# Selective-scan kernel: both sums of the softplus moved from VectorE to TensorE and PSUM

## The chip, the cores and the metric
The kernel runs on one core of one Trainium2 chip. The time is the device time of that core in microseconds (us). Five engines run their own instruction streams and meet through semaphores: TensorE (PE, matmuls), VectorE (DVE), ScalarE (ACT), GpSimd (POOL) and SyncE (SP, which starts DMAs).

## The reference, cut to what matters
A Mamba layer (8 sequences of 512 tokens, width 256, state 16) is followed by a layer norm and a mixture of 8 experts. What the change touches is `dt`, one number per token and channel, and what reads it:

```
dt = softplus(x_conv @ dt_w.T + dt_b)           # softplus(v) = relu(v) + ln(1 + exp(-|v|))
dA = exp(dt * A)                                # 16 states per channel
h  = h * dA + (dt * B) * x                      # the scan over tokens
y  = sum over states of h * C  + x * D
```

The kernel adds a correction to the logarithm. With e = exp(-|v|) it rounds t = e + 1 and keeps rest = (t - 1) - e, so that dt = relu(v) + ln(t) - rest. Three arrays of 128x1024 (two halves of 128 channels beside each other, 512 tokens each) therefore have to be summed for every sequence: `relu`, `logp` and `rest`.

## The kernel before, in words
**Stages.** Stage 1 computes the Mamba layer, the norms and the routing, one sequence at a time, and lasts until about 580 us. Stage 2 runs the experts, tile by tile, and stage 3 is the last norm. Only stage 1 is touched.

**Rounds and slots.** Stage 1 is a loop over rounds `r.like` = -1 (`FIRST`) to 9 (`LAST`), and in a round over 16 slots `t`, one for each state (`SLOTS`, `for r in ROUNDS: for t in range(SLOTS)`). Every engine walks through the same rounds and slots in its own function (`pe_stage1`, `act_stage1`, `dve_stage1`, `pool_stage1`) and issues in each slot what belongs to it. This order is written by hand; nothing else plans it. The engines are not in the same slot at the same time: each goes on as far as its semaphores allow. In round k four sequences are at work: part `a` prepares sequence k+1 (projections, convolution, softplus), part `b` scans sequence k, part `c` projects and norms sequence k-1, and part `d` routes sequence k-2. Part `c` starts in round 1, part `d` in round 2. `FIRST` has part `a` alone, round 7 has no part `a`.

**The scan.** In slot t DVE multiplies the drive by B (`weigh_inputs`, L1042, twice) and scans (`scan`, L1051, twice); POOL multiplies the state of slot t-1 by C (`read_state`, L1187, into `read`); PE adds the `read` of slot t-2 into `p_y` through the identity (`sum_states`, L640); ACT makes the decays of slot t+2 (`decays`, L824). The drive itself, `p_u` = dt * x_conv, is one DVE instruction in slot 15 (`drive`, L1033), and slot 0 of the next round reads it.

**The softplus of sequence k+1 in round k.** ACT stores |v| and relu(v) in slot 8 (L789, L790), then B and C (`store_bc`, L815), computes exp and t in slot 9 (L796, L800) and the logarithm in slot 10 (L806; it loads another table for it). DVE computes `rest` in slot 11 (`softplus_rest`, L1011), adds relu and logp in slot 12 (`add_log`, L1018), and subtracts `rest` in slot 13 (`scan_inputs`, L1025), which gives `dt`. POOL's `while_scanning` waits in slots 11, 12, 13 and 15 for these four DVE instructions before it goes on to its own `read_state`. In `FIRST` the same is done once, before the first scan.

**PSUM banks.** Every product of parts a, c and d goes through one of two banks in turn (`Round.blocks` lists them in order). PE fills a bank, signals `bank_full`, ACT or DVE copies it out and signals `bank_read`; PE may fill it again when the block before in that bank is read.

**What else stands near.** On ACT: the squares of the second norm (`variance`, L853) in slot 11, the copy of the gate's second half (`store_in`, L762) in slot 12, the second norm (`second_norm`, L861) in slot 13, the SiLU of the gate (`silu_gate`, L782) with two table loads in slot 14. On POOL: the power of the second norm (`power`, L1202 to L1206) in slot 12, and indirect DMAs that scatter rows (`scatter`, L1229) in slots 2 to 15, two of them at the start of slot 15. At the start of a round PE transposes and routes (`transpose_rows`, `route`), projects (`project`), counts (`count`, which DVE reads at L1106), projects out and convolves.

Of the kernel before, what the change touches and what calls it, by code (L numbers as in the profile page):

```python
# [53 lines left out]
class Round:  # L54
# [13 lines left out]
    def blocks(self):  # L68
        d, a, c = self.d, self.a, self.c
        return (["tr0", "tr1", "rt"] * d + ["in0", "in1"] * a + ["cnt"] * d + ["o0", "o1"] * c + ["cv0", "cv1"] * a  # L70
                + ["dt0", "dt1", "bc", "in2", "in3"] * a)

    def block(self, name):

# [79 lines left out]
def build(nc, ctx, ins, out):  # L154
    def sem(name):
        return ctx.enter_context(nc.semaphore(name))

    def sb(name, *shape, dt=F32, at=ctx):
        return at.enter_context(nc.sbuf_tensor(name, [P, *shape], dt))
# [23 lines left out]
    for name, *shape in SMALL:  # L183
# [39 lines left out]
    c_before, ones_f, b_out = set_up[:, 0:P], set_up[:, P:2 * P], set_up[:, 2 * P:2 * P + D]  # L223
    reorder = sb("reorder", P, at=one)
    table = sb("table", 1, at=one)
    rate_t = sb("rate_t", HALVES, P, at=one)
    rate = sb("scan_rate", HALVES, STATE, at=one)
    skip_w = sb("skip_w", HALVES, P, at=one)
# [46 lines left out]
    s_xt, s_x = sem("s_xt"), sem("s_x")  # L275
    bank_full = [sem(f"bank_full{i}") for i in range(2)]
    bank_read = [sem(f"bank_read{i}") for i in range(2)]
    s_silu, s_exp, s_log, s_rest0, s_rest, s_sum, s_dt, s_u = (
        sem(n) for n in ("s_silu", "s_exp", "s_log", "s_rest0", "s_rest", "s_sum", "s_dt", "s_u"))
    s_put = [sem(f"s_put{i}") for i in range(2)]  # L280
    s_rep = [sem(f"s_rep{i}") for i in range(RING)]
    s_order, s_decay, s_bu, s_state, s_read, s_added = (
# [284 lines left out]
    def pe_stage1(pe):  # L567
# [57 lines left out]
        def from_xc(r, name, at, n):  # L625
# [2 lines left out]
                pe.wait_ge(s_silu, 2 * r.s.at(1).n + 1)  # L628
            product(bank[0:n, :], columns(at, n), lambda k: xc[r.s.at(1).p][:, k, :]).then_inc(done, 1)

        def sum_states(s, t):

            n = SLOTS * s.n + t
            if t == 0:
                after(pe, s_y, s.n)
                for h in range(HALVES):
                    pe.matmul(p_y[h][:, :], skip_w[:, h, :], xc[s.p][:, h, :], start=True, stop=False)
            pe.wait_ge(s_read, n + 1)
            for h in range(HALVES):
                mm = pe.matmul(p_y[h][:, :], ident[:, :], read[:, t % 4, h, :], start=False, stop=(t == SLOTS - 1))  # L640
            mm.then_inc(s_added, 1)
# [49 lines left out]
        for r in ROUNDS:  # L691
            for t in range(SLOTS):
                if t < 2 and r.c:
                    sum_states(r.s.at(-1), SLOTS - 2 + t)
                if r.last and t == 0:
                    transpose_tile(pe, Seq(0, 0))
                    up_projection(pe, Seq(0, 0), 0)
                if r.d and t == 0:
                    transpose_rows(r, 0)
                    transpose_rows(r, 1)  # L700
                if r.d and t == 1:
                    route(r)
                if r.a and t == 2:
                    project(r, 0)
                    project(r, 1)
                if r.last and t == 4:
                    up_projection(pe, Seq(0, 0), 1)
                if r.d and t == (4 if r.last else 3):
                    count(r)
                if r.c and t == 3:  # L710
                    project_out(r, 0)
                    project_out(r, 1)
                if r.a and t == 4:
                    convolve(r, 0, range(TAPS))
                if r.a and t in (5, 6):
                    half = TAPS // 2 * (t - 5)
                    convolve(r, 1, range(half, half + TAPS // 2))
                if r.like == Round.FIRST and t == 5:
                    order_rate()
                if r.a and t == 8:  # L720
                    for i in range(HALVES):
                        from_xc(r, f"dt{i}", DT_ + i * P, P)
                    from_xc(r, "bc", BC, 2 * STATE)
                if r.like == Round.FIRST and t == 9:
                    place_rate()
                if r.a and t in (10, 11):
                    project(r, t - 8)
                if t >= 2 and r.b:
                    if t == 2 and r.like == 0:
                        pe.wait_ge(s_set_dve, SET_DVE)  # L730
                    sum_states(r.s, t - 2)


    def act_stage1(act):
# [49 lines left out]
        def store_dt(r, h):  # L784

            bank, done = full(act, r, f"dt{h}")
            if h == 0 and r.b:
                act.wait_ge(s_dt, r.s.n + 1)
            act.activation(relu[:, h, :], bank[:, :], ACT.Relu, bias=b_dt[:, h:h + 1])  # L789
            act.activation(expo[:, h, :], bank[:, :], ACT.Abs, bias=b_dt[:, h:h + 1]).then_inc(done, 1)  # L790

# [23 lines left out]
            act.activation(bc_out[0:2 * STATE, :], bank[0:2 * STATE, :], ACT.Identity, bias=b_bc2[0:2 * STATE, 0:1])\  # L815
               .then_inc(done, 1)

        def decays(s, t):

            after(act, s_state, halves_done(s, t - AHEAD))  # L820
            if t == 0:
                act.wait_ge(s_dt, s.n + 1)
            for h in range(HALVES):
                act.activation(decay[t % AHEAD][:, h, 1:LEN], dt[s.p][:, h, 1:LEN], ACT.Exp, scale=rate[:, h, t:t + 1])\  # L824
                   .then_inc(s_decay, 1)
# [43 lines left out]

        def store_x1t(r, k):  # L870
            bank, done = full(act, r, f"tr{k}")
            act.wait_ge(s_sum, SEQS if not r.a else r.s.n + 1)
            act.activation(x1t[:, k, :], bank[:, :], ACT.Copy).then_inc(done, 1)

        def router_exp(r):
# [4 lines left out]
        for r in ROUNDS:  # L880
            for t in range(SLOTS):
# [15 lines left out]
                if r.a and t in (11, 12):  # L897
                    store_in(r, t - 9)
                if r.a and t == 14 and r.b:
                    silu_gate(r)  # L900
                if r.like == 0 and t == 2:
                    silu_gate(Round(r.s.at(-1), Round.FIRST))

                if r.like == Round.FIRST and t == SLOTS - 1:
                    act.wait_ge(s_set_dve, SET_DVE)
                    for i in range(AHEAD - 2):
                        decays(r.s.at(1), i)
                if r.b and t < SLOTS - AHEAD + 2:
                    decays(r.s, t + AHEAD - 2)
                if r.next_b and r.b and t >= SLOTS - AHEAD + 2:  # L910
                    decays(r.s.at(1), t - SLOTS + AHEAD - 2)
                if r.a and r.b and t == 10:
                    softplus_log(r)

# [65 lines left out]
    def dve_setup_rest(dve):  # L980
        dve.memset(neg_half[:, :], -0.5)
        for i, value in enumerate((-1.0 / (16 * D), -1.0 / D, EPS)):
            dve.memset(norm_c[:, i, :], value)
        dve.tensor_copy(base[:, :], c_queue[:, :])
        dve.tensor_scalar(lower[:, :, :], lower[:, :, :], -SMALLEST, None, ALU.mult)
        dve.tensor_copy(before[:, :], c_before)
        dve.tensor_copy(ones[:, :], ones_f)
        dve.memset(scrap[:, 2:3], 0.0).then_inc(s_left, 1)
        dve.memset(chosen[:, :, :], 0.0)
        for h in range(HALVES):  # L990
            dve.tensor_scalar(skip_w[:, h, :], ident[:, :], skip[:, h:h + 1], None, ALU.mult)
        for h in range(2):
            last = dve.memset(rows[h][:, :, :], 0.0)
        last.then_inc(s_set_dve, 1)
        for i in range(AHEAD):
            last = dve.memset(decay[i][:, :, 0:1], 0.0)
        last.then_inc(s_set_dve, 1)
# [6 lines left out]
    def dve_stage1(dve):  # L1004
# [6 lines left out]
            dve.scalar_tensor_tensor(flat(rest[:, :, :]), flat(rest[:, :, :]), -1.0, flat(expo[:, :, :]),  # L1011
                                     ALU.add, ALU.subtract).then_inc(s_rest, 1)

        def add_log(r):

            s = r.s.at(1)
            dve.wait_ge(s_log, s.n + 1)
            dve.tensor_tensor(flat(relu[:, :, :]), flat(relu[:, :, :]), flat(logp[:, :, :]), ALU.add).then_inc(s_sum, 1)  # L1018

        def scan_inputs(r):  # L1020

            s = r.s.at(1)
            dve.wait_ge(s_sum, s.n + 1)
            dve.wait_ge(s_rest, s.n + 1)
            dve.tensor_tensor(flat(dt[s.p][:, :, :]), flat(relu[:, :, :]), flat(rest[:, :, :]), ALU.subtract).then_inc(s_dt, 1)  # L1025

        def drive(r):

            s = r.s.at(1)
            dve.wait_ge(s_dt, s.n + 1)  # L1030
            dve.wait_ge(s_silu, 2 * s.n + 1)
            after(dve, s_bu, halves_done(s, -1))
            dve.tensor_tensor(p_u[:, :], flat(dt[s.p][:, :, :]), flat(xc[s.p][:, :, :]), ALU.mult).then_inc(s_u, 1)  # L1033
# [88 lines left out]
        for r in ROUNDS:  # L1122
            for t in range(SLOTS):
# [36 lines left out]
                    dve.tensor_copy(index[r.s.at(-2).p][:, :], flat(spot_sum[:, :, :])).then_inc(s_index, 1)  # L1160
                if r.a and t == (11 if r.b else 10):
                    softplus_rest(r)
                if r.a and t == (12 if r.b else 10):
                    add_log(r)
                if r.like == Round.FIRST and t == 11:
                    negate_rate(dve)
                if r.a and t == 13:
                    scan_inputs(r)
                if r.c and t == 9:
                    residual(r)  # L1170
                if r.a and t == SLOTS - 1:
# [7 lines left out]
    def pool_stage1(pool):  # L1179
# [57 lines left out]
        def while_scanning(r, t):  # L1237
# [5 lines left out]
                pool.wait_ge(s_index, r.s.at(-2).n + 1)  # L1243
            if r.a and t == 11:
                pool.wait_ge(s_rest, r.s.at(1).n + 1)
            if r.a and t == 12:
                pool.wait_ge(s_sum, r.s.at(1).n + 1)
            if r.c and t == 9:
                pool.wait_ge(s_residual, r.s.at(-1).n + 1)
            if r.a and t == 13:  # L1250
                pool.wait_ge(s_dt, r.s.at(1).n + 1)
            if r.a and t == 15:
                pool.wait_ge(s_u, r.s.at(1).n + 1)

# [446 lines left out]
```

## Time and profile before

| what | value |
|---|---|
| median of 3 timed runs | 1333.25 us (1333.24 to 1339.11) |
| the profiled execution's own time | 1337.31 us |
| its span, first to last instruction | 1335.5 us |
| mean granted clock of TensorE | 0.941 |
| busy: PE, DVE, ACT, POOL | 88%, 79%, 67%, 56% of the span |
| drive of the first sequence starts | 39.30 us |
| drive of the seventh (last in round 6) starts | 506.60 us |

Times in the rows are microseconds from the start of the span. A matmul of f32 shows as two records, so that 8 records of L640 are the four matmuls of two slots. Records of neighbouring instructions overlap a little, because a record includes the tail of an instruction; the distance of two starts is what an instruction takes in a full queue. "Idle before" in square brackets is the time that the engine stood still before the row, with the instruction that ended it.

### The profile page before, as it was taken

To read this page: it belongs to the slowest core of one execution; us is meant where nothing else is said; L and a number is where in the kernel's file an instruction comes from. 1 tells how busy PE (TensorE), PEld (TensorE's weight loads), DVE (VectorE), ACT (ScalarE), POOL (GpSimd) and SP (SyncE) were. 2 spreads that over 40 slices of the span, in tenths; PEclk is the share of its full clock that TensorE was granted. 3 is DMA by queue.
4 is the path that set the end of the run, shared out by engine and by line. 5 is a ranking of instruction groups with operands and counts; after the bars stand their busy time and mean duration, and the time that the engine had idled before them with its cause. 6 is when DMAs were issued, how large, how long until landed. Compare 5 with 4: busy or idle time off the path is not lost. (4 is left out here: it accounts for less than half of the span.)

```text
span 1335.5 us, 17897 instructions
## 1 busy us (share of the span) xinstructions
PE 1170.2 (88%) x5138; PEld 805.3 (60%) x5138; DVE 1048.7 (79%) x1791; ACT 896.6 (67%) x1551; POOL 745.3 (56%) x566
## 2 busy tenths in 40 slices
PE   7879897979898897676899999999999999999940
PEld 3324353534353434245788888888888888888830
DVE  2999999999999999964777667777677777766734
ACT  3785959495959585516577766777676777766734
POOL 0356567888787878967633444443444433444442
PEclk9899998999999898977899999999999999999975
DMA  2543444445454545354866556556556566556637
GB/s 74 217 179 127 154 148 177 176 166 187 173 191 172 192 154 181 127 192 157 315 164 161 133 139 165 160 162 162 128 140 167 160 162 163 138 135 161 162 36 252
DMA packets 69260, 217.21 MB, mean 163 GB/s; under 512 B 7520, under 2 KB 43232, under 8 KB 56288
## 3 DMA queue, kind: packets, MB, share of 16 engines
q1 hardware_dynamic: 29664, 167.42, 34.4%
q0 software_dynamic: 26880, 36.72, 16.1%
q10 hardware_dynamic: 12672, 12.58, 2.9%
q8 instruction: 16, 0.26, 0.1%
q14 instruction: 28, 0.23, 0.0%
HBM read 165.54 MB, written 51.15 MB: 162 GB/s over the span
## 5 line engine op out<-in xcount | busy, mean ns | idle before, releaser
L640 PE MATMUL p_y<-read,small 128*128 128x512 f32 x512 | 257.8, 642 | 58.2 <-POOL read L1187 58.2
L1051 DVE TENSOR_TENSOR_SCAN state<-decay,p_bu 128x512 f32<-128x512 f32 x256 | 297.3, 1203 | 1.5 <-issue 1.5
L1511 POOL DMA_INDIRECT total<-o_v,tok x144 | 267.4, 1857 | 44.1 <-issue 44.0
L640 PEld LDWEIGHTS p_y<-read,small 128*128 128x128 f32 x512 | 101.3, 205 | 199.5 <-issue 116.8
L1509 POOL TENSOR_TENSOR scrap<-neg_half 128x1 f32<-128x1 f32 x36 | 13.6, 379 | 319.9 <-ACT o_v L1418 317.3
L824 ACT ACTIVATE decay<-dt,scan_rate 128x511 f32<-128x511 f32 x256 | 164.3, 710 | 10.1 <-DVE state L1051 9.8
L504 ACT ACTIVATE gate_v<-p_g,bias 128x512 f32<-128x512 f32 x144 | 98.4, 683 | 102.8 <-PE p_up L494 97.7
L1229 POOL DMA_INDIRECT queues<-rows,index x128 | 133.4, 1042 | 32.5 <-issue 29.2
L1405 ACT ACTIVATE ah<-a_v 128x512 fp32r<-128x512 f32 x144 | 91.1, 633 | 89.6 <-DVE a_v L518 85.9
L1187 POOL TENSOR_TENSOR read<-state,bc 128x1024 f32<-128x1024 f32 x64 | 127.5, 2004 | 20.7 <-DVE p_bu L1042 8.4
L512 DVE TENSOR_SCALAR up_v<-up_v 128x512 f32<-128x512 f32 x144 | 61.4, 427 | 68.5 <-ACT up_v L507 65.9
L1456 DVE TENSOR_TENSOR al<-a_v,ah 128x512 fp32r<-128x512 f32 x144 | 98.8, 686 | 12.4 <-ACT ah L1405 12.4
L518 DVE SCALAR_TENSOR_TENSOR a_v<-gate_v,up_v 128x512 f32<-128x512 f32 x144 | 99.7, 693 | 4.9
L507 ACT ACTIVATE up_v<-p_up,bias 128x512 f32<-128x512 f32 x144 | 98.2, 682 | 0.0
L1187 POOL TENSOR_TENSOR read<-state,first_wh 128x1024 f32<-128x1024 f32 x32 | 64.0, 2001 | 59.6 <-DVE p_bu L1042 53.8
L1187 POOL TENSOR_TENSOR read<-state,first_wl 128x1024 f32<-128x1024 f32 x32 | 63.9, 1997 | 39.9 <-DVE p_bu L1042 15.6
L1378 PE MATMUL p_o<-first_wh,ah 128*128 128x256 f32 x288 | 82.6, 287 | 2.3 <-DVE al L1456 2.3
L1378 PE MATMUL p_o<-wh,ah 128*128 128x256 f32 x288 | 81.9, 284 | 1.7 <-DVE al L1456 1.7
L1042 DVE TENSOR_TENSOR p_bu<-p_u,bc 128x512 f32<-128x512 f32 x128 | 81.3, 681 | 0.0
L1378 PE MATMUL p_o<-first_wl,ah 128*128 128x256 f32 x288 | 80.8, 281 | 0.0
L1378 PE MATMUL p_o<-first_wh,al 128*128 128x256 f32 x288 | 80.8, 281 | 0.0
L1378 PE MATMUL p_o<-wh,al 128*128 128x256 f32 x288 | 80.3, 279 | 0.0
(220 smaller groups left out, 3017.6 us busy)
## 6 DMA issues: line engine op xcount, KB each, us to landing
bc<-bc_rows SPq DMA_DIRECT2D x32, 1024.0 KB, 4.7
first_raw<-in_w_experts SPq DMA_DIRECT2D x19, 1668.0 KB
raw_w<-in_w_experts SPq DMA_DIRECT2D x18, 1668.0 KB
first_wh<-bc_rows SPq DMA_DIRECT2D x16, 1024.0 KB
first_wl<-bc_rows SPq DMA_DIRECT2D x16, 1024.0 KB
first_rows<-queues SPq DMA_DIRECT2D x19, 544.0 KB
xq<-queues SPq DMA_DIRECT2D x18, 544.0 KB
queues<-pad SPq DMA_DIRECT2D x9, 544.0 KB
```

The lines of the kernel that those rows point to most:

```text
L504: act.activation(gate_v[i % 2][:, :], p_g[i % 2][:, :], ACT.Silu, bias=bias[t.p][:, 0, i:i + 1], scale=ALPHA)
L507: act.activation(up_v[i % 2][:, :], p_up[i % 2][:, :], ACT.Identity, bias=bias[t.p][:, 1, i:i + 1])\
L518: dve.scalar_tensor_tensor(a_v[i % 2][:, :], gate_v[i % 2][:, :], TOP, up_v[i % 2][:, :], ALU.min, ALU.mult)\
L640: mm = pe.matmul(p_y[h][:, :], ident[:, :], read[:, t % 4, h, :], start=False, stop=(t == SLOTS - 1))
L824: act.activation(decay[t % AHEAD][:, h, 1:LEN], dt[s.p][:, h, 1:LEN], ACT.Exp, scale=rate[:, h, t:t + 1])\
L1051: dve.tensor_tensor_scan(state[t % 4][:, h, :], decay[t % AHEAD][:, h, :], p_bu[:, h * LEN:(h + 1) * LEN], 0.0, ALU.mult, ALU.add).then_in ...
L1187: pool.tensor_tensor(read[:, t % 4, :, :], state[t % 4][:, :, :], of_state(t, 1), ALU.mult).then_inc(s_read, 1)
L1229: pool.indirect_dma_start(queues, bass.IndirectOffsetOnAxis(ap=index[s.p][:, i:i + 1], axis=0), rows[s.p][:, i // TOPK, :], None).then_inc ...
L1378: mm = pe.matmul(to, v[:, i, a * P:(a + 1) * P], w[t.p][:, c:c + D], start=(i == 0 and a % 2 == 0 and m == 0), stop=(i == CH - 1 and m == ...
L1405: act.activation(ah[:, i, :], a_v[i % 2][:, :], ACT.Copy).then_inc(s_ah, 1)
L1456: dve.tensor_tensor(al[:, i, :], a_v[i % 2][:, :], ah[:, i, :].bitcast(F32), ALU.subtract).then_inc(s_al, 1)
L1511: pool.indirect_dma_start(total, bass.IndirectOffsetOnAxis(ap=tok[t.p][:, a:a + 1], axis=0), o_v[t.p][:, a, :], None, compute_op=ALU.add). ...
```

## The change
DVE no longer adds. For each half PE runs three matmuls into a bank (two new blocks `sp0` and `sp1`): the identity times relu, the identity times logp, and minus the identity (`minus`, a new constant) times rest. It does so in slots 12 and 13, before that slot's `sum_states`. ACT copies both banks to `dt` in slot 14, and `silu_gate` moves from slot 14 to 15. DVE's drive, ACT's first decays and POOL wait accordingly: the semaphores `s_sum` and `s_dt` are gone, and with them POOL's waits in slots 12 and 13.

```diff
@@ blocks
-                + ["dt0", "dt1", "bc", "in2", "in3"] * a)
+                + ["dt0", "dt1", "bc", "in2", "in3", "sp0", "sp1"] * a)
@@ pe_stage1
+        def add_softplus(r, h):
+
+            s = r.s.at(1)
+            bank, done = block(r, f"sp{h}")
+            pe.wait_ge(s_log, s.n + 1)
+            if h == 0 and r.like == Round.FIRST:
+                pe.wait_ge(s_set_dve, SET_DVE)
+            pe.matmul(bank[:, :], ident[:, :], relu[:, h, :], start=True, stop=False)
+            pe.matmul(bank[:, :], ident[:, :], logp[:, h, :], start=False, stop=False)
+            pe.wait_ge(s_rest, s.n + 1)
+            pe.matmul(bank[:, :], minus[:, :], rest[:, h, :], start=False, stop=True).then_inc(done, 1)
@@
                 if r.a and t in (10, 11):
                     project(r, t - 8)
+                if r.a and t in (12, 13):
+                    add_softplus(r, t - 12)
@@ act_stage1: store_dt and store_x1t lose their waits on s_dt and s_sum
+        def store_sum(r, h):
+
+            s = r.s.at(1)
+            bank, done = full(act, r, f"sp{h}")
+            act.activation(dt[s.p][:, h, :], bank[:, :], ACT.Copy).then_inc(done, 1)
@@
-            if t == 0:
-                act.wait_ge(s_dt, s.n + 1)
+            if summed:
+                for h in range(HALVES):
+                    bank, n = summed.block(f"sp{h}")
+                    act.wait_ge(bank_read[bank], n)
@@
                 if r.a and t == 14 and r.b:
+                    store_sum(r, 0)
+                    store_sum(r, 1)
+                if r.a and t == 15 and r.b:
                     silu_gate(r)
@@
                 if r.like == Round.FIRST and t == SLOTS - 1:
                     act.wait_ge(s_set_dve, SET_DVE)
+                    store_sum(r, 0)
+                    store_sum(r, 1)
@@ dve_setup_rest
+        dve.tensor_scalar(minus[:, :], ident[:, :], -1.0, None, ALU.mult)
@@ dve_stage1: add_log (L1018) and scan_inputs (L1025) are gone
         def drive(r):
 
             s = r.s.at(1)
-            dve.wait_ge(s_dt, s.n + 1)
+            for h in range(HALVES):
+                bank, n = r.block(f"sp{h}")
+                dve.wait_ge(bank_read[bank], n)
@@ while_scanning (POOL)
-            if r.a and t == 12:
-                pool.wait_ge(s_sum, r.s.at(1).n + 1)
-            if r.a and t == 13:
-                pool.wait_ge(s_dt, r.s.at(1).n + 1)
```

## Rows read from the trace of the kernel before

**Rows 1.** The page's first part: busy time, share of the span, instructions.
```profile
PE 1170.2 (88%) x5138; PEld 805.3 (60%) x5138; DVE 1048.7 (79%) x1791; ACT 896.6 (67%) x1551; POOL 745.3 (56%) x566
```

**Rows 2.** Windows: length, busy PE, PEld, DVE, ACT, POOL, granted clock, DMA.
```profile
38.00:40.00 2.00, 1.75 (x3) 0.34 (x1) 1.97 (x4) 1.04 (x4) 0.00 (x0) 0.72 0.85 360
...
280.00:340.00 60.00, 52.80 (x153) 25.88 (x152) 57.84 (x81) 42.05 (x78) 48.63 (x38) 0.94 0.52 183
```

**Rows 3.** Waits of DVE, 230 to 437 us: total, times, longest.
```profile
DVE place L1106 <- PE p_bank L686: 2.6, 3, 0.9
DVE rest L1011 <- ACT rest L800: 2.1, 3, 0.7
```

**Rows 4.** Timeline of DVE: start, length, instruction, idle before.
```profile
39.30 1.23 DVE L1033 TENSOR_TENSOR p_u<-dt,xc 128x1024 f32<-128x1024 f32 x1
...
96.67 1.23 DVE L1033 TENSOR_TENSOR p_u<-dt,xc 128x1024 f32<-128x1024 f32 x1
...
162.41 1.23 DVE L1033 TENSOR_TENSOR p_u<-dt,xc 128x1024 f32<-128x1024 f32 x1
...
230.18 2.04 DVE L1033 TENSOR_TENSOR p_u<-dt,xc 128x1024 f32<-128x1024 f32 x1
...
355.76 1.23 DVE L1018 TENSOR_TENSOR first_raw<-first_raw,x1t 128x1024 f32<-128x1024 f32 x1 [0.16 <-ACT x1t L806]
356.90 2.32 DVE L1051 TENSOR_TENSOR_SCAN state<-decay,p_bu 128x512 f32<-128x512 f32 x2
...
360.32 1.22 DVE L1025 TENSOR_TENSOR dt<-first_raw,rest 128x1024 f32<-128x1024 f32 x1
...
368.52 2.05 DVE L1033 TENSOR_TENSOR p_u<-dt,xc 128x1024 f32<-128x1024 f32 x1
```

**Rows 5.** Timeline of POOL, columns as before.
```profile
154.88 0.60 POOL L1202 TENSOR_TENSOR rstd<-var,norm_c 128x4 f32<-128x4 f32 x1 [1.88 <-ACT squares L853]
...
360.99 0.60 POOL L1202 TENSOR_TENSOR rstd<-var,norm_c 128x4 f32<-128x4 f32 x1 [1.88 <-ACT squares L853]
...
365.49 3.97 POOL L1187 TENSOR_TENSOR read<-state,bc 128x1024 f32<-128x1024 f32 x2
369.63 1.80 POOL L1229 DMA_INDIRECT queues<-rows,index  x1 [0.17 <-issue]
371.73 0.98 POOL L1229 DMA_INDIRECT queues<-rows,index  x1 [0.30 <-DVE state L1051]
372.74 3.96 POOL L1187 TENSOR_TENSOR read<-state,bc 128x1024 f32<-128x1024 f32 x2
...
430.04 0.60 POOL L1202 TENSOR_TENSOR rstd<-var,norm_c 128x4 f32<-128x4 f32 x1 [1.88 <-ACT squares L853]
```

**Rows 6.** Timeline of PE, columns as before.
```profile
33.07 6.68 PE L597 MATMUL p_bank<-first_raw,w 128*128 128x512 f32 x8
...
100.08 5.58 PE L640 MATMUL p_y<-read,small 128*128 128x512 f32 x8 [2.85 <-POOL read L1187]
...
356.77 5.31 PE L640 MATMUL p_y<-read,small 128*128 128x512 f32 x12
367.56 6.69 PE L640 MATMUL p_y<-read,small 128*128 128x512 f32 x8 [5.47 <-POOL read L1187]
374.80 1.98 PE L640 MATMUL p_y<-read,small 128*128 128x512 f32 x4 [0.54 <-POOL read L1187]
...
552.93 1.98 PE L640 MATMUL p_y<-read,small 128*128 128x512 f32 x4 [2.83 <-POOL read L1187]
```

**Rows 7.** Timeline of ACT, columns as before.
```profile
348.19 0.68 ACT L815 ACTIVATE bc_out<-p_bank,b_bc 32x512 f32<-32x512 f32 x1 [0.84 <-PE p_bank L597]
...
360.82 0.67 ACT L762 ACTIVATE sg<-p_bank,small 128x512 f32<-128x512 f32 x1
...
363.84 2.06 ACT L861 ACTIVATE rows<-z,neg_mean,rstd 128x256 f32<-128x256 f32 x4
...
377.25 1.08 ACT L873 ACTIVATE x1t<-p_bank 128x512 f32<-128x512 f32 x2 [3.90 <-PE p_bank L664]
```

More of the change, by code:

```diff
@@ L225, in build @@
     table = sb("table", 1, at=one)
+    minus = sb("minus", P, at=one)
     rate_t = sb("rate_t", HALVES, P, at=one)
@@ L277, in build @@
     bank_read = [sem(f"bank_read{i}") for i in range(2)]
-    s_silu, s_exp, s_log, s_rest0, s_rest, s_sum, s_dt, s_u = (
-        sem(n) for n in ("s_silu", "s_exp", "s_log", "s_rest0", "s_rest", "s_sum", "s_dt", "s_u"))
+    s_silu, s_exp, s_log, s_rest0, s_rest, s_u = (
+        sem(n) for n in ("s_silu", "s_exp", "s_log", "s_rest0", "s_rest", "s_u"))
     s_put = [sem(f"s_put{i}") for i in range(2)]
@@ L786, in store_dt @@
             bank, done = full(act, r, f"dt{h}")
-            if h == 0 and r.b:
-                act.wait_ge(s_dt, r.s.n + 1)
             act.activation(relu[:, h, :], bank[:, :], ACT.Relu, bias=b_dt[:, h:h + 1])
@@ L816, in store_bc, with decays @@
                .then_inc(done, 1)
-        def decays(s, t):
+        def store_sum(r, h):
+            s = r.s.at(1)
+            bank, done = full(act, r, f"sp{h}")
+            act.activation(dt[s.p][:, h, :], bank[:, :], ACT.Copy).then_inc(done, 1)
+        def decays(s, t, summed=None):
             after(act, s_state, halves_done(s, t - AHEAD))
-            if t == 0:
-                act.wait_ge(s_dt, s.n + 1)
+            if summed:
+                for h in range(HALVES):
+                    bank, n = summed.block(f"sp{h}")
+                    act.wait_ge(bank_read[bank], n)
             for h in range(HALVES):
@@ L871, in store_x1t @@
             bank, done = full(act, r, f"tr{k}")
-            act.wait_ge(s_sum, SEQS if not r.a else r.s.n + 1)
             act.activation(x1t[:, k, :], bank[:, :], ACT.Copy).then_inc(done, 1)
@@ L905, in act_stage1 @@
                     act.wait_ge(s_set_dve, SET_DVE)
+                    store_sum(r, 0)
+                    store_sum(r, 1)
                     for i in range(AHEAD - 2):
-                        decays(r.s.at(1), i)
+                        decays(r.s.at(1), i, r if i == 0 else None)
                 if r.b and t < SLOTS - AHEAD + 2:
@@ L910, in act_stage1 @@
                 if r.next_b and r.b and t >= SLOTS - AHEAD + 2:
-                    decays(r.s.at(1), t - SLOTS + AHEAD - 2)
+                    decays(r.s.at(1), t - SLOTS + AHEAD - 2, r if t == SLOTS - AHEAD + 2 else None)
                 if r.a and r.b and t == 10:
@@ L1012, in softplus_rest @@
                                      ALU.add, ALU.subtract).then_inc(s_rest, 1)
[L1014 to L1025, printed above, removed]
         def drive(r):
             s = r.s.at(1)
-            dve.wait_ge(s_dt, s.n + 1)
+            for h in range(HALVES):
+                bank, n = r.block(f"sp{h}")
+                dve.wait_ge(bank_read[bank], n)
             dve.wait_ge(s_silu, 2 * s.n + 1)
@@ L1162, in dve_stage1 @@
                     softplus_rest(r)
-                if r.a and t == (12 if r.b else 10):
-                    add_log(r)
                 if r.like == Round.FIRST and t == 11:
                     negate_rate(dve)
-                if r.a and t == 13:
-                    scan_inputs(r)
                 if r.c and t == 9:
@@ L1245, in while_scanning @@
                 pool.wait_ge(s_rest, r.s.at(1).n + 1)
-            if r.a and t == 12:
-                pool.wait_ge(s_sum, r.s.at(1).n + 1)
             if r.c and t == 9:
                 pool.wait_ge(s_residual, r.s.at(-1).n + 1)
-            if r.a and t == 13:
-                pool.wait_ge(s_dt, r.s.at(1).n + 1)
             if r.a and t == 15:
```

## The prediction
> **What bounds the kernel now.** I read the page's shares first. TensorE is busy most over the whole span [rows 1], but the change touches stage 1 alone, so I took windows there: from 280 to 340 us DVE is busy 57.8 of 60 us and PE 52.8 [rows 2]. That looks like a stage bound by DVE, and the change takes two instructions from DVE. So I asked what DVE still waits for. In three rounds it waits at L1106 for PE's count (2.6 us together) and at L1011 for ACT (2.1 us) [rows 3]. A sole bound waits for nobody; these waits say that another chain sets the pace. I followed it backwards through the timelines of the round around 368 us.
>
> - POOL starts the power of the second norm (L1202) at 360.99 after waiting for ACT's squares, then works without a wait for DVE until its read of slot 14, at 372.74; PE's sum of that read starts at 374.80 [rows 5, 6]: 13.8 us.
> - From there PE works through the start of the next round with a single wait, for ACT, until ACT can store B and C. That is the counterpart, one round later, of ACT's row at 348.19 [rows 7]. The period is 69.05 us (L1202 at 360.99 and at 430.04 [rows 5]), so this part takes 348.19 + 69.05 - 374.80 = 42.4 us.
> - ACT then works without a pause to the squares' end: 360.99 - 348.19 = 12.8 us.
>
> The three parts close a loop of 69.05 us in which DVE has no work. DVE's drive goes at the same pace, 138.3 us for two rounds (230.18 to 368.52) [rows 4], because DVE waits for this loop. Only the first rounds, with fewer parts, are DVE's: 57.4, 65.7 and 67.8 us (39.30, 96.67, 162.41, 230.18 [rows 4]).
>
> **What is removed.** L1018 takes 1.1 us to the next start (355.76 to 356.90) and 0.16 of waiting, L1025 1.1: 2.4 us of DVE per round, 2.3 in round 0 [rows 4]. In rounds 3 to 6 that is time of an engine off the loop. One thing reaches it: L1202 takes 0.60 us where the same kind of POOL instruction takes 0.20, since it starts at 360.99 while L1025 (360.32 to 361.54) runs [rows 4, 5]. I count 0.4 us less for the loop at most. POOL's freed waits in slots 12 and 13 buy nothing, because right after them it waits 1.88 us for ACT's squares [rows 5].
>
> **What is added on PE.** An f32 matmul of 128x512 is two records of 0.43 us at full clock (12 records in 5.31 us, the last one's tail left out) [rows 6]: 0.86 us. Six are 5.15 us per round. In slots 12 and 13 PE has its only long pause, 5.47 us before 367.56, and after it runs 8 records at 1.2 GHz in 6.69 us instead of 3.6 [rows 6]. So the time is covered: sp0 runs about 358.5 to 361.1, sum 10 to 362.8, sp1 (its bank is read at 361.5 by the copy that starts at 360.82 [rows 7]) to 365.4, sum 11 to 367.1. Behind the new waits on PE stand only these sums; logp, rest and banks are there when PE comes. POOL's read needs a sum three slots back, which is there too.
>
> **What is added on ACT.** Two copies of a bank take 1.08 us with the last one's tail, as L873's two do [rows 7]. They stand behind the second norm, which ends at 365.9 [rows 7], so dt is ready near 367.0. DVE, 2.5 us earlier than 368.52, is at its drive at 366.0 and waits 1.0 us; behind it stand the last scan and the next round. ACT's later silu_gate is harmless: its 3.6 us with both table loads end before DVE needs the second decay, about 4 us spare.
>
> **The drive and POOL.** The drive takes 2.05 us at 368.52 and 1.23 in the early rounds [rows 4]. POOL's two reads run 365.49 to 369.46 [rows 5]; from there 1.13 us lead to 370.6, the drive's end. The DMA at 369.63 takes 1.80 instead of 0.98 and starts inside the drive [rows 4, 5]. So each stands until the other is through. In the new kernel the drive is ready at 367.0 and the second read at 367.1: whichever comes first, the other stands, and POOL's part becomes 0.1 to 0.4 us shorter, no more. The Trainium skill says the same under "SBUF — State Buffer", Who interferes with whom: a DVE instruction with two SBUF inputs and a GpSimd instruction that reads SBUF lock each other out, the second one blocking fully. By that rule as by the rows, an earlier drive can't pass a read that has started.
>
> **What is added at the start.** In FIRST nothing covers the matmuls. PE's projections end at 39.75 us and all else was ready by 38 [rows 6]. The clock has come back to 2.4 GHz within 38 to 40 us (0.72 on average [rows 2]), after a stretch of dense matmuls. Six matmuls: 5.15, two copies of which one lies beside PE: 0.7, semaphores 0.2. The drive starts near 45.6 instead of 39.30 [rows 4]: +6.3 us. At half clock it would be +11.
>
> **PE's clock at the start of the burst.** This is the unknown. Before, the slow stretch was over when sum 14 started at 374.80, after 0.54 us of pause [rows 6]. Now sums 12 and 13 run at full clock and end near 370.9, and sum 14 waits for POOL's read until about 374.5: a pause of 2.8 to 3.6 us, just ahead of the 42 us in which PE sets the loop. Nearest rows: after 2.85 us of pause 8 records took 5.58 us instead of 3.6 (2.0 lost), after 2.83 us four took 1.98 (none lost), after 5.47 eight took 6.69 (3.1 lost) [rows 6]. So 0 to 3.1 us per round; I take 1.1, between the two rows at the nearest pause and nearer the loss.
>
> **The sum**, against the profiled execution's 1337.31: start +6.3; round 0 -2.3; round 1 -1.5 (the drive follows ACT, whose dt is ready 6.0 us after L1202, where the drive came 7.5 after it, 154.88 to 162.41 [rows 4, 5]); round 2 follows that drive, 0; rounds 3 to 6 each -0.25 + 1.1 = +0.85, together +3.4; round 7 and the stage's end follow, -0.3 for the drive's earlier end. That is +5.6; I say +5, since the first late burst may still find slack. The median of the runs is 4 us below the profiled execution, with one run of three near it, so I put the difference on the median: 1333.25 + 5 = 1338 us.
>
> **Rivals.**
> 1. *DVE is the bound after all.* For it: 57.8 of 60 us [rows 2]. Against it: the waits [rows 3] and the closed loop. Then seven rounds save 2.4 and the start costs 6.3: -10.5, 1323 us. "Perfetto Trace Analysis", Optimizing Scalar/DVE Operations, in the Trainium skill, speaks for it: with DVE saturated, moving work to ScalarE may help. The loop says that here DVE isn't what to relieve.
> 2. *The clock falls before every burst and stays down as after the long pause.* Place: rounds 3 to 6 and round 7's start. Price 3.1 per round: +2.5 + 4 x 2.85 = +14, 1347 us. It decides against the kernel from about 1.3 us lost per round. For it: the pause at 100.08; against it: the one at 552.93 [rows 6].
> 3. *The clock holds*: +2.5 - 1.0 - 0.3 = +1, 1334 us.
>
> **How the numbers follow.** Forecast (a fall in some rounds, 1335 to 1341): 0.42. Rival 3: 0.16. Rival 2, with halfway cases: 0.24. Rival 1, whole or in part: 0.18. A change of under 0.5% (6.7 us) can't be told from none. Slower by more (over 1339.9): rival 2 and a quarter of the forecast, 0.35. Faster by more (under 1326.6): most of rival 1, 0.16. The rest, 0.49, is within. The range takes in the holding clock, most of rival 2 and half of rival 1: 1324 to 1347.
>
> **What would show it.** The first drive near 45.6 us. Drives in rounds 3 to 6 about 69 to 71 us apart, not 66.6. DVE waiting at L1033 for ACT's copy, and longer at L1106. PE without the 5.47 us pause, but with one of about 3 us before sum 14, and 1.2 GHz after it in some rounds. L1202 at 0.20. It would be wrong if the rounds came at 67 us (DVE was the bound), or the first drive before 44.

## The result: 0.7% slower

In nine runs each the changed kernel took 1345.5 us (median; 1339.04 to 1350.41) and the kernel before 1338.34 (1333.24 to 1341.28). The ratio is 1.0069, with a 95% interval of 1.0050 to 1.0088: about 9 us slower. A second set of runs of the same two kernels gave 1.0074 (1.0052 to 1.0096). The forecast was 5 us slower and "within 0.5%". Every ratio is taken against the kernel before in runs on the same chip.

From one execution to the next the kernel before varies by 8 us and the changed one by 11, about as much as the change is worth, so absolute positions differ between profiles. I compare distances: from one drive to the next, and from the last drive to stage 3.

### The profile page after: what moved, and what is told of

The parts are those of the page before. It is cut to its first block and busy times, and to the rows that moved or that the text cites. A ratio compares the mean times of both kernels' runs of the same rounds, so it can differ in the third digit from the quotient of the medians.

```text
span 1339.5 us, 18069 instructions
## 1 busy us (share of the span) xinstructions
PE 1200.1 (90%) x5234; PEld 820.3 (61%) x5234; DVE 1036.4 (77%) x1776; ACT 905.9 (68%) x1567; POOL 741.2 (55%) x566
## 5 line engine op out<-in xcount | busy, mean ns | idle before, releaser
L653 PE MATMUL p_y<-read,small 128*128 128x512 f32 x512 | 252.6, 626 | 37.4 <-POOL read L1198 37.3
L653 PEld LDWEIGHTS p_y<-read,small 128*128 128x128 f32 x512 | 97.4, 197 | 172.5 <-issue 107.3
```

## The profile after

The page's first part: PE has more work and DVE a little less. This answers to [rows 1]. The mean granted clock of TensorE rose from 0.941 to 0.952, although the kernel is slower: what counts here is where the clock falls.

```profile
PE 1200.1 (90%) x5234; PEld 820.3 (61%) x5234; DVE 1036.4 (77%) x1776; ACT 905.9 (68%) x1567; POOL 741.2 (55%) x566
```

DVE's drives, after. They answer to [rows 4].

```profile
41.58 1.23 DVE L1048 TENSOR_TENSOR p_u<-dt,xc 128x1024 f32<-128x1024 f32 x1 [9.31 <-issue]
...
227.07 3.19 DVE L1048 TENSOR_TENSOR p_u<-dt,xc 128x1024 f32<-128x1024 f32 x1 [1.10 <-ACT dt L835]
...
297.37 3.20 DVE L1048 TENSOR_TENSOR p_u<-dt,xc 128x1024 f32<-128x1024 f32 x1 [1.11 <-ACT dt L835]
...
365.97 3.19 DVE L1048 TENSOR_TENSOR p_u<-dt,xc 128x1024 f32<-128x1024 f32 x1 [1.10 <-ACT dt L835]
...
436.26 3.19 DVE L1048 TENSOR_TENSOR p_u<-dt,xc 128x1024 f32<-128x1024 f32 x1 [1.10 <-ACT dt L835]
```

The drive waits 1.1 us for ACT's copy of dt and then stands until POOL's reads are through. From 227.07 the periods are 70.3, 68.6 and 70.3 us, where the kernel before had 69.0 to 69.3. Why one is short shows on PE, here at sum 14, the `sum_states` of slot 14 with which PE opens the next round (the rows answer to [rows 6]):

```profile
304.79 1.98 PE L653 MATMUL p_y<-read,small 128*128 128x512 f32 x4 [3.29 <-POOL read L1198]
...
373.39 2.40 PE L653 MATMUL p_y<-read,small 128*128 128x512 f32 x4 [3.29 <-POOL read L1198]
```

and in the granted clock (window, length, busy PE, PEld, DVE, ACT, POOL, clock, DMA):

```profile
305.00:308.00 3.00, 3.00 (x14) 1.76 (x14) 3.00 (x5) 0.76 (x2) 3.00 (x2) 1.00 0.52 153
...
373.00:376.00 3.00, 2.61 (x6) 1.27 (x7) 3.00 (x5) 0.57 (x1) 3.00 (x3) 0.80 0.34 136
376.00:379.00 3.00, 3.00 (x11) 2.06 (x10) 3.00 (x5) 2.06 (x4) 3.00 (x2) 0.63 0.82 328
```

The pause is the same 3.29 us both times. After the first the clock stayed at 2.4 GHz and the round took 68.6 us; after the second it fell to 1.2 GHz once sum 14 had begun (on average 0.80 and then 0.63 of full speed), and the round took 70.3. POOL's rows answer to [rows 5]:

```profile
360.01 0.20 POOL L1213 TENSOR_TENSOR rstd<-var,norm_c 128x4 f32<-128x4 f32 x1 [3.31 <-ACT squares L874]
...
364.10 3.96 POOL L1198 TENSOR_TENSOR read<-state,bc 128x1024 f32<-128x1024 f32 x2
```

The power's first step takes 0.20 us where it took 0.60. POOL now waits 3.31 us for ACT's squares instead of 1.88: its freed waits bought nothing. Its two reads end at 368.06, and DVE's drive 1.10 us later. ACT's two copies took 1.06 us:

```profile
364.83 1.06 ACT L835 ACTIVATE dt<-p_bank 128x512 f32<-128x512 f32 x2
```

## The experiments

The ratios are against the kernel before on the same chip. after_again, before_again, first_dve and no_sums ran on one chip, and warm, tr_early, first_warm and first_warm_tr on another, where the change itself was not run; a comparison of one of these four with the change therefore goes over two ratios of different chips. The table gathers the periods of the drive in each profile (differences of the drives' starts), and what is left from the last drive to stage 3's first load (`sums`, issued by SP).

| kernel | first drive | round 0 | 1 | 2 | 3 | 4 | 5 | 6 | rest | ratio (95%) |
|---|---|---|---|---|---|---|---|---|---|---|
| before | 39.30 | 57.4 | 65.7 | 67.8 | 69.0 | 69.3 | 69.0 | 69.05 | 795.3 | |
| before_again | 36.31 | 57.4 | 65.75 | 67.8 | 69.0 | 69.3 | 69.0 | 69.0 | 789.3 | |
| after | 41.58 | 55.1 | 64.2 | 66.2 | 70.3 | 68.6 | 70.3 | 70.0 | 799.8 | 1.0069 (1.0050 to 1.0088) |
| after_again | 42.80 | 55.1 | 64.2 | 66.2 | 70.3 | 71.45 | 71.6 | 71.6 | 793.0 | 1.0074 (1.0052 to 1.0096) |
| first_dve | 35.94 | 55.1 | 64.2 | 66.2 | 71.5 | 71.6 | 71.6 | 71.65 | 792.2 | 1.0026 (1.0013 to 1.0038) |
| no_sums | 36.47 | 57.05 | 63.2 | 65.6 | 68.6 | 68.6 | 68.6 | 68.6 | 794.1 | 0.9933 (0.9914 to 0.9953) |
| warm | 41.71 | 55.1 | 64.2 | 66.2 | 68.6 | 68.6 | 68.6 | 68.6 | 797.9 | 0.9986 (0.9972 to 1.0000) |
| tr_early | 42.22 | 55.1 | 64.2 | 66.2 | 69.4 | 69.3 | 68.15 | 68.2 | 797.0 | 0.9991 (0.9978 to 1.0003) |
| first_warm | 35.95 | 55.1 | 64.2 | 66.2 | 68.65 | 68.6 | 68.6 | 68.6 | 795.8 | 0.9962 (0.9946 to 0.9978) |
| first_warm_tr | 36.91 | 55.1 | 64.2 | 67.6 | 68.2 | 68.2 | 68.2 | 68.2 | 797.5 | 0.9948 (0.9929 to 0.9967) |

### The two kernels once more (after_again, before_again)

No edit.

> The changed kernel once more, for a second profile and more times. Loop theory (the period of rounds 3 to 6 is set by PE, ACT and POOL in turn, and PE's clock falls after the pause of 3.3 us before sum 14 in most rounds, each fall costing 1.7 us): periods of the drive in rounds 3 to 6 are 68.6 where the granted clock stays up and 70.0 to 70.3 where it falls, and which rounds fall differs from the first profile. First drive: the first profile's 41.6 us came with a PE that was at full clock earlier than in the kernel before; if that is chance of the execution, it moves by up to 4 us here. DVE's wait of 6.6 us for something remote at the read of the counts near 631 us: if it is chance, it is not the same here; if it comes with the program's length, it is again 6 to 7 us. Time 5 to 10 us above before.

> The kernel before, once more, for a second profile. Loop theory: drive periods in rounds 3 to 6 69.0 to 69.3 whatever the clock does, because the half-speed stretch ends before sum 14. First drive between 37 and 41 us, depending on PE's clock from 20 to 35 us. DVE's wait for something remote near 626 us was 2.5 us; about the same if it belongs to the program, between 0 and 7 if it is chance.

Measured: the kernel before keeps its periods to 0.05 us; the changed one does not. The ratio is 1.0074, within the 5 to 10 us expected. In after_again three rounds took 71.5 to 71.6 us. There the clock had already fallen when PE resumed, and all of sum 14 ran at 1.2 GHz:

```profile
305.97 3.78 PE L653 MATMUL p_y<-read,small 128*128 128x512 f32 x4 [3.29 <-POOL read L1198]
```

3.78 us against 1.98, after the same 3.29 us of pause. A fall costs 1.4 to 1.7 us in some rounds and 2.9 to 3.0 in others, measured against 68.6. I had expected only the smaller kind.

The first drive of the kernel before came at 36.31, earlier than the 37 to 41 expected and 3.0 us earlier than in its first profile. In the first profile PE's clock had already fallen in the first `dt` projections, after the same 2.02 us of pause:

```profile
22.01 7.20 PE L597 MATMUL p_bank<-xc,w 128*128 128x512 f32 x12 [2.02 <-ACT xc L775]
...
21.07 5.51 PE L597 MATMUL p_bank<-xc,w 128*128 128x512 f32 x12 [2.02 <-ACT xc L775]
```

The first row is from before, the second from before_again. From this point the first drive is 17.29 us away in before and 15.24 in before_again; in after and after_again, whose projections took 5.51 us too, it is 20.98 away. At equal clocks the start therefore costs 5.7 us.

DVE's wait for something remote (6.6 us in the first profile of the change) is not in these two profiles, so it doesn't belong to the program alone.

### DVE's sums taken away (no_sums)

```diff
-            act.activation(relu[:, h, :], bank[:, :], ACT.Relu, bias=b_dt[:, h:h + 1])
+            act.activation(dt[r.s.at(1).p][:, h, :], bank[:, :], ACT.Relu, bias=b_dt[:, h:h + 1])
...
-                if r.a and t == (12 if r.b else 10):
-                    add_log(r)
-                if r.a and t == 13:
-                    scan_inputs(r)
```

With the two sums their waits go as well, on ACT and in slots 12 and 13 of POOL. What is left out is the logarithm and `rest`: they are computed and not used, and `dt` is relu(v) alone.

> The kernel before with both DVE sums left out and nothing put in their place: ACT writes relu(v) straight to dt, so the logarithm and the rest are computed and not used (the softplus is cut to its relu). It shows what DVE's 2.4 us per round are worth. Rival 1 (DVE is the bound): rounds 1 to 6 shorter by 2.4 each, about 17 us in rounds and 2.5 at the start, ratio 0.985. Loop theory: round 0 -2.3, rounds 1 and 2 -2.4 each at most, rounds 3 to 6 -0.4 each (68.6 to 68.9 us), start -2.5: about 9 to 10 us, ratio 0.993; drive periods in rounds 3 to 6 within 0.5 us of 69.

Measured: 0.9933 (0.9914 to 0.9953), where the loop theory said 0.993 and the DVE theory 0.985. Rounds 1 and 2 became 2.5 and 2.2 us shorter, and rounds 3 to 6 take 68.6 us each, as expected. The total is less of a confirmation than it looks, because round 0 missed: it saved 0.3 us instead of 2.3. In the profiled execution DVE's first scan waits for ACT's decays (the first row). In rounds 3 to 6 DVE comes to its drive earlier and just stands there longer:

```profile
40.88 2.33 DVE L1038 TENSOR_TENSOR_SCAN state<-decay,p_bu 128x512 f32<-128x512 f32 x2 [1.71 <-ACT decay L823]
...
290.90 4.15 DVE L1020 TENSOR_TENSOR p_u<-dt,xc 128x1024 f32<-128x1024 f32 x1
```

```profile
290.00 3.95 POOL L1170 TENSOR_TENSOR read<-state,bc 128x1024 f32<-128x1024 f32 x2
```

The first fence is DVE's timeline, the second POOL's. POOL's reads end at 293.95; 1.1 us later, at 295.05, the drive ends. So DVE is not the bound in rounds 3 to 6: 2.4 us of DVE per round, the freed waits included, buy 0.4 to 0.7 us.

### The first round by DVE (first_dve)

```diff
+                if r.like == Round.FIRST and t == 10:
+                    dve.wait_ge(s_log, 1)
+                    dve.tensor_tensor(flat(relu[:, :, :]), flat(relu[:, :, :]), flat(logp[:, :, :]), ALU.add)
...
+                if r.like == Round.FIRST and t == 13:
...
-            for h in range(HALVES):
-                bank, n = r.block(f"sp{h}")
-                dve.wait_ge(bank_read[bank], n)
+            if r.like == Round.FIRST:
+                dve.wait_ge(s_dt, 1)
```

The cut shows the heart of the edit; the blocks `sp0` and `sp1` of the first round and the waits that go with them are dropped too.

> Change as it is, but in the first round alone (before the first scan) DVE adds as in the kernel before; no sp blocks there. Theory: in the first round nothing hides six matmuls and two copies, so this returns what they cost: 5.15 + 1.2 - 2.4 - what was waiting anyway, 4 to 6 us off the changed kernel's time; ratio to before 1.002 to 1.004. Rival (the loss sits in the clock falls and in the stage change alone, and the start is slack): same time as the changed kernel, ratio 1.007.

Measured: 1.0026 (1.0013 to 1.0038), against 1.0074 (1.0052 to 1.0096) for the change on the same chip: 0.0048 of 1332 us, 6.4 us, with some 3 us of uncertainty either way. The first drive is at 35.94 instead of 42.80, 6.9 us apart; 1.1 us of that is only that PE began the projections earlier (20.69 against 21.82). From there to the drive it is 15.25 us against 20.98, so the uncovered matmuls and copies cost 5.7 us, within the 4 to 6 expected. The rounds of this profile are the worst of the three with the 3.29 us pause, four of four with the larger fall, 71.5 to 71.65 us.

### The pause filled (warm)

```diff
+                if t == 0 and 3 <= r.like <= SEQS - 1:
+                    bank, _ = block(r, "tr0")
+                    for i in range(3):
+                        pe.matmul(bank[:, :], ident[:, :], taps[:, 0:4, :].rearrange("p a b -> p (a b)"),
+                                  start=True, stop=True)
                 if t < 2 and r.c:
                     sum_states(r.s.at(-1), SLOTS - 2 + t)
```

> The changed kernel, and in rounds 3 to 7, ahead of sum 14, PE runs three matmuls of constants (2.6 us) into the bank that the transposes overwrite: work that serves nothing and fills most of the pause of 3.3 us. Clock theory (the pause makes the granted clock fall to 1.2 GHz at the start of PE's 42 us, 1.6 to 3.0 us each time): the clock stays up, drive periods in rounds 3 to 6 are 68.6 in every profile, 4 to 11 us off the changed kernel's time; ratio to before 1.000 to 1.003. Rival (more PE work is simply more time, the clock is no part of it): periods as before at 70 to 71.6 or longer, ratio 1.007 or more.

Measured: 0.9986 (0.9972 to 1.0000), where the change had 1.0069, and 1.0074 on the chip of the other group; I had expected 1.000 to 1.003. PE's timeline shows three matmuls that nobody reads, and the pause cut to 0.71 us:

```profile
299.73 2.74 PE L709 MATMUL p_bank<-taps,small 128*128 128x512 f32 x6
303.18 1.98 PE L653 MATMUL p_y<-read,small 128*128 128x512 f32 x4 [0.71 <-POOL read L1203]
```

```profile
295.76 3.20 DVE L1053 TENSOR_TENSOR p_u<-dt,xc 128x1024 f32<-128x1024 f32 x1 [1.10 <-ACT dt L840]
...
364.36 3.20 DVE L1053 TENSOR_TENSOR p_u<-dt,xc 128x1024 f32<-128x1024 f32 x1 [1.10 <-ACT dt L840]
```

DVE's drives, in the second fence, are 68.60 us apart, and those of the other three rounds are the same to 0.01 us. The kernel does more PE work than the change and is faster, by 0.8 to 0.9% if the two ratios are compared over the chips. The rival, that PE work is simply time, is out: what the change lost in rounds 3 to 6 was the clock. Those rounds account for 7.7 us (70.5 on average in the two profiles of the change, against 68.6), less than the 11 to 12 us between the ratios; where the rest comes from isn't shown.

### The transposes into the pause (tr_early)

```diff
+                if r.d and r.c and not r.last and t == 0:
+                    transpose_rows(r, 0)
+                    transpose_rows(r, 1)
                 if t < 2 and r.c:
                     sum_states(r.s.at(-1), SLOTS - 2 + t)
```

The two transposes are taken out of their old place, behind sum 14, in the same rounds.

> The changed kernel with the two transposes of slot 0 (0.9 us) put ahead of sum 14, into the pause; nothing is added. Loop theory: PE's part of the loop is shorter by 0.65 us, of which DVE's logits take some back: periods 68.2 to 68.4 where the clock holds; the pause shrinks to 2.4 us, after which it falls less often. Ratio to before 1.000 to 1.004. Rival (the loop isn't the bound): no change from 1.007.

Measured: 0.9991 (0.9978 to 1.0003), below the range I gave. The pause is 2.41 us; in two rounds the clock fell (69.4 and 69.3), in two it held (68.15 and 68.16). After the pause that opens round 7 it held as well. The two kinds on PE, the first with a fall:

```profile
304.51 5.27 PE L653 MATMUL p_y<-read,small 128*128 128x512 f32 x8 [2.41 <-POOL read L1201]
...
441.96 3.94 PE L653 MATMUL p_y<-read,small 128*128 128x512 f32 x8 [2.41 <-POOL read L1201]
```

Work taken out of PE's part of the loop shortens the round by 0.45 us (68.60 to 68.15). It goes below the 68.6 us at which both no_sums and the change with the clock held had stopped, so in those PE's part was in the bound.

### Put together (first_warm, first_warm_tr)

The edits above together; first_warm_tr has two matmuls of constants and then the transposes.

> first_dve and warm together: the start as before, and the pause filled with matmuls of constants. Sum of parts: start 0, rounds 0 to 2 -2.3, -1.6, -1.6, rounds 3 to 6 -0.45 each: -7.3 us, ratio 0.9945; if the parts don't add, nearer to 1.

> first_warm with two instead of three matmuls of constants and then the transposes, both ahead of sum 14. Sum of parts: another 0.3 to 0.5 us per round off in rounds 3 to 6, periods 68.1 to 68.4, ratio 0.992 to 0.994. If POOL's read of slot 15 or DVE's logits come last instead, no gain over first_warm.

Measured: 0.9962 (expected 0.9945) and 0.9948 (expected 0.992 to 0.994). The rounds 3 to 6 are as forecast, 68.6 and 68.16. Both kernels gained a little less in time than the sum of the parts; for first_warm_tr that lies within the interval (0.9929 to 0.9967), for first_warm just outside it (0.9946 to 0.9978). first_warm_tr is faster than the kernel before by 0.5%.

Round 2 of first_warm_tr took 1.35 us more than that of the other kernels with the new sums (67.57 against 66.2). The moved transposes are not the reason: tr_early moves them in that round too, and its round 2 took 66.20. What differs is the granted clock, as PE's row and a window of first_warm_tr show:

```profile
166.98 5.38 PE L598 MATMUL p_bank<-first_raw,w 128*128 128x512 f32 x8
168.00:171.00 3.00, 3.00 (x5) 1.11 (x4) 2.86 (x10) 0.62 (x1) 1.15 (x2) 0.53 0.05 19
```

In tr_early the same eight records took 1.96 and 1.98 us, with the clock at 1.00. Here the clock fell although PE had just paused for only 0.47 and 0.26 us.

## Why the prediction was wrong

The direction and the mechanism were as predicted; one term of the sum, the clock's, was much too small.

- *DVE isn't the bound; PE, ACT and POOL close a loop.* Right, and shown by runs from both sides: no_sums takes DVE's work away and gains 0.4 to 0.7 us per round; tr_early takes 0.9 us of PE's out of the loop and gains 0.45. The working itself proved less than it seemed: PE's 42.4 us were found from the period and the ends of the other two parts, so the three had to add up to 69.05.
- *The start costs 6.3 us.* Nearly right: 5.7 at equal clocks. The position I gave, 45.6, was off (41.58 and 42.80), because I added to 39.30, a start with PE's clock fallen. I had named a first drive before 44 as a sign of being wrong; it came, and it was the position that was wrong and not the cost.
- *Round 0 -2.3, round 1 -1.5.* Measured -2.3 and -1.6.
- *Round 2: 0.* Wrong: -1.6. Its loop still starts at DVE's drive, and the next drive again comes sooner after ACT's squares (227.07 - 221.11 = 6.0 us after POOL's first step, instead of 7.5). I had counted that gain once where it comes twice.
- *Rounds 3 to 6: -0.25 without a fall.* Measured -0.5 (68.6 against 69.0 to 69.3).
- *The clock: +1.1 per round, and none for round 7.* This is the step that failed. The pause itself was foreseen (2.8 to 3.6 us; it is 3.29), but its price was not. I took a value between a row with 2.0 us lost and a row with none [rows 6], as if the two were equally likely. The same trace had two more pauses of that length, and the clock fell after both:

```profile
158.87 5.23 PE L640 MATMUL p_y<-read,small 128*128 128x512 f32 x8 [2.89 <-POOL read L1187]
...
560.01 2.50 PE L640 MATMUL p_y<-read,small 128*128 128x512 f32 x4 [2.79 <-POOL read L1187]
```

At full clock these take 3.6 and 1.98 us. So the clock fell after three of the four pauses of 2.79 to 2.89 us. In the 12 rounds of after, after_again and first_dve it fell 11 times, 4 times at 1.4 to 1.7 us and 7 times at 2.9 to 3.05; the mean over the 12 is 2.3 us (1.9 over the eight of after and after_again). Round 7, which I had at -0.3, pays too: its sum 14 also begins after 3.29 us of pause, and the clock fell there in all three profiles. From its drive to the end of that sequence's last sum it took 75.2 and 76.6 us in the change against 73.7 and 73.2 before, and 74.2 to 74.9 where the pause was filled: about 2.4 us more than before, and about 1.4 more than with the pause filled, which is roughly what the clock cost there.

With these sizes the sum is 5.7 - 2.3 - 1.6 - 1.6 - 2.0 + 4 x 2.3 + 2.4 = +9.8 us (8.2 with 1.9), against 9.2 and 9.9 measured. The agreement is one of means: the rounds of the change's two profiles alone differ by 5.7 us together. What came about lies between my forecast and rival 2, "the clock falls before every burst and stays down": the fall came nearly every time, at 2.3 us and not 3.1. I had given rival 2, with such halfway cases, 0.24. I named the granted clock as the unknown; but a pause that reaches every round's critical stretch should have been priced near its upper row.

## What to carry to other kernels

Before relieving the busiest engine, see whether it still waits for somebody: DVE was busy 96% of the window from 280 to 340 us, and 2.4 us of it per round were worth 0.5. When work is moved on TensorE, ask what pauses it leaves and what runs right after them. The kernel before had pauses of 5.47 us, and the slow matmuls behind them had slack; the change had 3.29 us right ahead of the bounding stretch, and lost up to 3 us per round there. Matmuls that compute nothing were the cheaper choice. A mean of the granted clock doesn't show this: it rose while the time grew. Work that is hidden in the steady loop isn't hidden in the first round, so that round may keep its own way.

## What the runs showed of the hardware

- The same pause of 3.29 us gave three outcomes in 12 rounds: the clock held (once), fell soon after PE resumed (4 times, a loss of 1.4 to 1.7 us), or fell before it did (7 times, 2.9 to 3.05). After 2.41 us it fell in two of four rounds, after 0.7 in none of twelve. The length of the pause alone doesn't decide it: after the same 2.02 us before the first `dt` projections it fell in two of ten profiles (7.20 us for twelve records, against 5.51), and in round 2 of first_warm_tr it fell after 0.47 and 0.26 us.
- A DVE instruction with two SBUF inputs that meets GpSimd's reads stands until they end: 1.23 us alone, 3.19 in the change, 4.15 in no_sums. From round 2 on it ended 1.1 us after POOL's second read in all ten profiles. POOL had a second read queued right behind the first, and DVE didn't get in between.
- From the last drive to stage 3 the profiles differ by up to 10 us (789.3 to 799.8), 6.8 of them between two executions of the same changed kernel. In half of them DVE waits for something remote at the reading of the last counts: 2.5 us in before, 6.6 in after, 7.3, 7.2 and 7.4 in warm, tr_early and first_warm_tr, none in the other five. What that is stays open; it may be part of why the kernels' runs spread by 8 to 11 us.
